# The skip term of a long convolution, moved from a matmul over channels to the diagonal of products that lie in SBUF

## What is computed

```python
kv = vr[:, :, :, None, :] * x2r[:, :, None, :, :]
y = irfft(rfft(kv, n=2*L) * rfft(k, n=2*L)[None, :, None, None, :], n=2*L)[..., :L]
skip = bias.reshape(H, num_heads)[None, :, :, None, None]
y = y + kv * skip
out = jnp.einsum('bhijl,bhil->bhjl', y, x1r)      # x1 = x2 = ctx
x = x + out.reshape(B, D, L)
```

## Time and profile before

| | |
|---|---|
| median of 3 runs | 1346.17 us |
| the profiled execution | 1338.81 us, of which its span 1337.0 us |
| mean granted TensorE clock | 0.946 of 2.4 GHz; 1.00 from 40 to 600 us |
| stage A | to about 620 us |
| busy over the span | TensorE 87%, VectorE 60%, GpSimd 51%, ScalarE 40% |

### The profile page before, as it was taken

The page is one execution under the profiler, slowest core; times in us unless marked ns, Lnnn a source line. Parts: engine busy times, 40 slices in busy tenths (PEclk is TensorE's granted clock), DMA queues, the critical chain, the costliest instruction groups (busy, mean ns, idle before and its releaser), DMA issues. The chain is left out here.

```text
span 1337.0 us, 18158 instructions
## 1 busy us (share of the span) xinstructions
PE 1165.7 (87%) x5305; PEld 881.9 (66%) x5305; DVE 799.4 (60%) x1240; ACT 533.2 (40%) x980; POOL 687.4 (51%) x388
## 2 busy tenths in 40 slices
PE   3999999999999999998689999998878787878770
PEld 2767777777777777766589899965545454545450
DVE  1687777877777877776579955535333343334340
ACT  5455555555555555543212122134323233323330
POOL 5987889888898888880000000022334443444432
PEclk9999999999999999999799999999888899889985
DMA  6222333233333223312483344459999999899973
GB/s 187 83 72 77 98 98 95 74 85 88 98 98 87 84 75 98 98 50 57 99 245 105 107 119 112 111 167 289 248 247 261 251 270 270 215 266 259 258 184 39
DMA packets 87546, 194.73 MB, mean 146 GB/s; under 512 B 17888, under 2 KB 22688, under 8 KB 87392
## 3 DMA queue, kind: packets, MB, share of 16 engines
q1 hardware_dynamic: 73184, 158.76, 39.9%
q0 software_dynamic: 14336, 35.66, 13.2%
HBM read 150.55 MB, written 43.79 MB: 145 GB/s over the span
## 5 line engine op out<-in xcount | busy, mean ns | idle before, releaser
L937 POOL TENSOR_TENSOR ring<-vT,cT 128x1024 f32<-128x1024 f32 x128 | 249.0, 1955 | 79.5 <-ACT vT L710 52.9
L390 PE MATMUL Y<-split,toep 128*128 128x512 f32 x576 | 250.4, 435 | 9.4 <-POOL split L945 9.4
L1056 DVE TENSOR_TENSOR z<-Y,cT 128x1024 f32<-128x1024 f32 x128 | 156.1, 1219 | 126.0 <-PE Y L394 90.3
L945 POOL TENSOR_TENSOR split<-ring,split 128x1024 fp32r<-128x1024 f32 x96 | 229.7, 2393 | 0.4 <-ACT split L720 0.4
L392 PE MATMUL Y<-split,toep 128*128 128x512 f32 x576 | 228.5, 397 | 0.0
L391 PE MATMUL Y<-split,toep 128*128 128x512 f32 x576 | 228.3, 396 | 0.0
L981 POOL DMA_INDIRECT stage<-xn_rows,idx_i x64 | 71.5, 1117 | 299.6 <-issue 282.4
L608 PE MATMUL Y<-ring,xT 128*128 128x384 f32 x512 | 209.8, 537 | 0.5 <-DMA ring<-in_L_ffn_down_proj_dram 0.5
L1061 DVE TENSOR_REDUCE o<-z 128x128 f32<-128x1024 f32 x128 | 154.4, 1206 | 1.1
L521 PE MATMUL Y<-split 128*128 128x384 f32 x768 | 152.2, 347 | 1.6 <-DVE split L1115 1.6
L390 PEld LDWEIGHTS Y<-split,toep 128*128 128x128 f32 x576 | 109.2, 190 | 39.5 <-issue 19.1
(11 more groups left out here) (135 smaller groups left out, 1736.4 us busy)
## 6 DMA issues: line engine op xcount, KB each, us to landing
ring<-_L_ffn_gate_up_proj_dram SPq DMA_DIRECT2D x64, 768.0 KB
ring<-in_L_ffn_down_proj_dram SPq DMA_DIRECT2D x64, 384.0 KB
gr<-filters SPq DMA_DIRECT2D x32, 512.0 KB, 3.7
stage<-in_x_dram SPq DMA_DIRECT2D x32, 256.0 KB, 3.5
stage<-in_ctx_dram SPq DMA_DIRECT2D x32, 256.0 KB, 3.7
x_rows<-stage SPq DMA_DIRECT2D x32, 256.0 KB, 2.9
xn_rows<-xn SPq DMA_DIRECT2D x32, 256.0 KB, 3.0
xn<-xn_rows SPq DMA_DIRECT2D x32, 256.0 KB, 3.7
```

The source lines that it names most:

```text
L390: pe.matmul(y, high, kv[:, s, 0, a, n], start=(a == 0), stop=False)
L937: pool.tensor_tensor(to.rearrange("p (b j i) -> p b j i", i=NH, j=NH), a, d, ALU.mult).then_inc(kvp_ready, 1)
L945: pool.tensor_tensor(kv[:, s, 1, c, :], kvp[c], kv[:, s, 0, c, :].bitcast(F32), ALU.subtract).then_inc(kv_ready, 1)
L1056: dve.tensor_tensor(zz[c % 2].rearrange("p (b j i) -> p b j i", j=NH, i=NH), YY[c % 2][:, :].rearrange("p (b j i) -> p b j i", j=NH, i=NH) ...
```

## The change

The skip sum is no longer made by TensorE. The products that GpSimd has already written to SBUF hold, at every ninth of 64 columns, the products with equal heads. VectorE multiplies these diagonals by the skip values, into `w` (`diagonals`, once for chunks 0 to 2 and once for chunk 3), sums each eight (`v_ctx`, now on VectorE), multiplies by `cT` (`skip_term`, now in SBUF) and adds the result to the whole of `o` before it is transposed (`add_skip`). GpSimd's `v_ctx`, ScalarE's `skip_block`, TensorE's skip matmul and VectorE's `residual` go. `xr` is loaded straight from `x` by a DMA (`load_residual`), together with the skip values, behind the two stores and so ahead of the next load of filters. `load_tile` waits for `cT_ps` in place of `xr_ready`. GpSimd's products wait for the diagonals of the tile before, since these read the buffers that it writes. The copy of `six_scores` becomes a multiplication by 1.0. The three product buffers are laid into one strided tensor.

```diff
+            def load_residual(h, s):
+                if not among(h, 0, 1):
+                    sp.wait_ge(x1_ready, h - 1)
+                load_skip(h, s)
+                sp.dma_start(xr[:, s, :], rows(x_f, h)).then_inc(xr_in[s], 16)
             def load_tile(h, s):
-                sp.wait_ge(xr_ready, h - 1)
+                sp.wait_ge(cT_ps, h - 1)
                 load_rows(h, s)
-                load_skip(h, s)
...                                                   (SyncE, iteration)
                     store(h - 1, 1 - s)
+                if not among(h, NT - 1):
+                    load_residual(h + 1, 1 - s)
...                                                   (TensorE, transposes, turn_o)
-                pe.wait_ge(w_ready, h + 1)
-                pe.wait_ge(skip_ready, h + 1)
-                pe.matmul(DX[:, :], skip_b[:, s, :], w[:, s, :], start=True, stop=True).then_inc(dx_ps, 1)
-                pe.wait_ge(o_done, h * NC + NC)
+                pe.wait_ge(o_whole, h + 1)
...                                                   (ScalarE)
-                act.activation(skip_b[:, s, :], same_b, ACT.Copy, scale=skip_c[:, s, :]).then_inc(skip_ready, 1)
...                                                   (GpSimd, product and v_ctx)
                     if not among(h, 0):
+                        pool.wait_ge(diag_ready, h * 2 - 1)
                         pool.wait_ge(kv_ready, (h - 1) * (NC - 1) + c + 1)
-                pool.tensor_tensor(w[:, s, :], v[:, s, :], ct[:, s, :], ALU.mult).then_inc(w_ready, 1)
...                                                   (VectorE)
+            def diagonals(h, s, last):
+                dve.wait_ge(kvp_ready, h * NC + (NC if last else NC - 1))
...
+                n, c = (1, NC - 1) if last else (NC - 1, 0)
+                products = kv3[s].unsqueeze(1) if last else kvp_all
+                products = products.rearrange("p c (b n) -> p c b n", b=B)[:, :, :, 0:NH * NH:NH + 1]
+                skips = skip_c[:, s, :].unsqueeze(1).unsqueeze(1).to_broadcast([P, n, B, NH])
+                dve.tensor_tensor(w[:, s, c * P:(c + n) * P].rearrange("p (c b i) -> p c b i", c=n, i=NH),
+                                  products, skips, ALU.mult).then_inc(diag_ready, 1)
+            def v_ctx(h, s):
+                dve.tensor_reduce(vct[:], w[:, s, :].rearrange("p (n i) -> p n i", i=NH), AX.X, ALU.add).then_inc(vct_ready, 1)
             def skip_term(h, s):
-                dve.tensor_tensor(DX[:, :], DX[:, :], ct[:, s, :], ALU.mult).then_inc(dc_ready, 1)
-            def residual(h, s):
-                dve.tensor_tensor(xr[:, s, :], DX[:, :], xt[:, s, :], ALU.add).then_inc(xr_ready, 1)
+                dve.tensor_tensor(w[:, s, :].rearrange("p (n i) -> p n i", i=NH),
+                                  cT[:, s, :, :].rearrange("p c (b i) -> p (c b) i", i=NH),
+                                  vct[:].unsqueeze(2).to_broadcast([P, NC * B, NH]), ALU.mult).then_inc(skip_ready, 1)
+            def add_skip(h, s):
+                dve.wait_ge(o_done, h * NC + NC)
+                dve.wait_ge(skip_ready, h + 1)
+                whole = o[:, s, :, :].rearrange("p c n -> p (c n)")
+                dve.tensor_tensor(whole, whole, w[:, s, :], ALU.add).then_inc(o_whole, 1)
...                                                   (VectorE, six_scores)
-                dve.tensor_copy(s6[:, 0:K], s8[:, 0:K]).then_inc(s6_ready, 1)
+                dve.tensor_scalar(s6[:, 0:K], s8[:, 0:K], 1.0, None, ALU.mult).then_inc(s6_ready, 1)
...                                                   (VectorE, iteration)
                     total(h - 1, 1 - s, 3)
+                    add_skip(h - 1, 1 - s)
                 times(h, s, 0)
                 if prev2:
                     best_scores(h - 2)
-                if nxt:
-                    skip_term(h + 1, 1 - s)
+                diagonals(h, s, False)
                 total(h, s, 0)
                 times(h, s, 1)
+                diagonals(h, s, True)
                 if prev2:
                     six_scores(h - 2)
                 if prev:
                     add_x1(h - 1, 1 - s)
-                if nxt:
-                    residual(h + 1, 1 - s)
...
+                v_ctx(h, s)
                 times(h, s, 2)
+                skip_term(h, s)
                 total(h, s, 2)
```

More of the change, by code:

```diff
@@ L95, in build @@
         kv = split[:].rearrange("p (s a c n) -> p s a c n", s=2, a=2, c=NC)
-        kvp = [ring[:, 3, 0:KVC], ring[:, 3, KVC:2 * KVC], ring[:, 0, SI * NC:]]
-        kv3 = [ring[:, 1, SI * NC:], ring[:, 2, SI * NC:]]
+        kvp_all = ring[:, 0:NC - 1, SI * NC:]
+        kvp = [kvp_all[:, n, :] for n in range(NC - 1)]
+        kv3 = [ring[:, 3, 0:KVC], ring[:, 3, KVC:2 * KVC]]
         z = sb("z", [P, 4, 512])
@@ L473, in iteration @@
                 if not among(h, 0):
-                    if not among(h, NT - 1):
-                        pe.wait_ge(xr_ready, h + 2)
-                    else:
+                    if not among(h, 1):
+                        pe.wait_ge(sc_ready, h - 1)
+                    if among(h, NT - 1):
                         pe.wait_ge(sh_lo, 2)
@@ L762, in iteration @@
                 if nxt:
-                    skip_block(h + 1, 1 - s)
                     filter_blocks(h + 1, 1 - s)
@@ L1061, in total @@
                 dve.tensor_reduce(o[:, s, c, :], zz[c % 2].rearrange("p (n i) -> p n i", i=NH), AX.X, ALU.add).then_inc(o_done, 1)
-            def skip_term(h, s):
-                dve.wait_ge(dx_ps, h + 1)
-                dve.tensor_tensor(DX[:, :], DX[:, :], ct[:, s, :], ALU.mult).then_inc(dc_ready, 1)
-            def residual(h, s):
-                dve.wait_ge(dc_ready, h + 1)
-                if not among(h, 0, 1):
-                    dve.wait_ge(x1_ready, h - 1)
-                dve.tensor_tensor(xr[:, s, :], DX[:, :], xt[:, s, :], ALU.add).then_inc(xr_ready, 1)
+            def diagonals(h, s, last):
+                dve.wait_ge(kvp_ready, h * NC + (NC if last else NC - 1))
+                if not last:
+                    dve.wait_ge(skip_in[s], landed(h, s, 16))
+                    if not among(h, 0, 1):
+                        dve.wait_ge(o_whole, h - 1)
+                n, c = (1, NC - 1) if last else (NC - 1, 0)
[4 more added lines that the diff above has]
+                                  products, skips, ALU.mult).then_inc(diag_ready, 1)
@@ new lines, in v_ctx @@
+            def v_ctx(h, s):
+                dve.wait_ge(diag_ready, h * 2 + 2)
+                if not among(h, 0):
+                    dve.wait_ge(skip_ready, h)
+                dve.tensor_reduce(vct[:], w[:, s, :].rearrange("p (n i) -> p n i", i=NH), AX.X, ALU.add).then_inc(vct_ready, 1)
+            def skip_term(h, s):
+                dve.wait_ge(vct_ready, h + 1)
+                dve.tensor_tensor(w[:, s, :].rearrange("p (n i) -> p n i", i=NH),
+                                  cT[:, s, :, :].rearrange("p c (b i) -> p (c b) i", i=NH),
+                                  vct[:].unsqueeze(2).to_broadcast([P, NC * B, NH]), ALU.mult).then_inc(skip_ready, 1)
@@ L1129, in iteration @@
                     best_scores(h - 2)
-                if nxt:
-                    skip_term(h + 1, 1 - s)
-                else:
+                diagonals(h, s, False)
+                if not nxt:
                     shared_low(0)
@@ L1168, in _ @@
                 shift1(h)
-                if h == 0:
-                    skip_term(0, 0)
-                    residual(0, 0)
             dve.wait_ge(small_in, 16)
@@ L1255, in _ @@
             total(NT - 1, 1, 3)
+            add_skip(NT - 1, 1)
             scores(NT - 2)
```

34 lines of the change are left out of this document (10 added, 24 removed).

## The result

| | us | to the kernel before |
|---|---|---|
| before | 1346.16 (median of 4) | |
| after | 1419.55 (median of 4, 1415.87 to 1421.73) | 1.0557 (1.0509 to 1.0605) |
| forecast | 1373 (1320 to 1398) | |

What follows compares the result with a forecast made beforehand. Stage A was taken as bounded by TensorE's list and VectorE's cycle with GpSimd port waits. 16.3 + 0.1 + 1.0 + 2.15 = 19.55, taken as 19.4 us against 18.5, +27 us over 30 tiles: 1373 us, range 1320 to 1398.

Steps and rivals of the forecast that it cites:

- the cycles: Stage A's two limits per tile: TensorE's list, 17.8 us falling to 16.95, and VectorE's, 19.48 falling to 16.3 without port waits.
- the port: VectorE instructions reading SBUF by two routes wait for GpSimd's running instruction to end; at most 2.4 us each.
- Rival 2: No lock for tensor_tensor: 16.95 to 17.7 us per tile, middle 1310 us; chance 0.17 together with late filters bounding stage A.
- rival 1: The lock holds but `six_scores` gets through: 18.1 to 18.8 us per tile, 1334 to 1356 us; chance 0.36.
- the price of the step: Extra VectorE time for diagonals reading one column in nine, bounded at 0 to 0.5 us per tile.
- `six_scores` in full: On VectorE, `six_scores` lets GpSimd go first and waits for a whole product or low part: 2.15 us.
- the wait of the second diagonals: VectorE's diagonals over 128 columns wait for GpSimd's first or second product: 1.0 us, between 0.2 and 1.9.
- the step of nine: VectorE's diagonals read one column in nine: 0.1 us per tile in the forecast, 0.5 kept for the range.
- the cycle as laid out: VectorE's cycle in stage A: 16.3 us without port waits, plus 0.1, 1.0 and 2.15, giving 19.55 us per tile.
- changing phases: Stage A's tile taken as 19.4 instead of 19.55 us, as phases would differ from tile to tile.
- a stall was priced at its length: TensorE idle ahead of L407 over 2 us per tile, with no added price for a slower clock.
- Filters: SyncE loads filters 1.3 us plus 0 to 1 us later, moving GpSimd's start to 5.4 to 6.4 us; no cost by itself.

Runs made afterwards that it cites:

- after_six_reduce: The changed kernel with `six_scores` made by a tensor_reduce over one element instead of the multiplication by 1.0: 1353.2 us, 1.006 to before.
- after_filled_stall: The changed kernel with twelve overwritten 512-column matmuls added ahead of `turn_xn`, where TensorE waits for `xn`: 1396.0 us, 1.035 to before.
- after_filters_first: The changed kernel with only SyncE's order changed, skip values and `xr` loaded behind the filters: 1409.7 us, 1.041 to before.

## Why the prediction was right and where it failed

**Right: the cycles.** The list of TensorE without the skip matmul, 16.95 us, was reached (16.9). That the copy of six columns holds the kernel before at 18.5 us was read from ends that coincide, and taking it out gave the 17.8 us of the undisturbed tile.

**Right: the port.** All of it was argued from one instruction of six columns. The experiments show it for tensor_tensor with two fp32 inputs in SBUF, by the operand (1777 to 393 ns) and by the moment (1616 to 389 ns), and show that the multiplication by 1.0 waits as the copy did. The rule of the Trainium skill that the prediction named ("SBUF — State Buffer", Who interferes with whom) agrees with the durations shown here, down to the blocked GpSimd instruction (2.85 us for 2.41). Rival 2, no lock, falls; rival 1, `six_scores` getting through, too. Its other half held once the instruction was mended: `after_six_reduce` had 18.8 us, rival 1 with the price of the step 18.7 to 18.8. That they meet so closely is in part luck: the 18.8 us contain the low clock of some tiles (granted clock 0.98 from 100 to 550 us), which rival 1 did not have either.

**Right: `six_scores` in full.** Forecast 2.15 us of wait, measured 2266 - 149 = 2.12 us.

**Mis-sized: the wait of the second diagonals.** Put at 1.0 us between bounds of 0.2 and 1.9; measured 1777 - 390 = 1.39 us. The middle of the bounds was no better than a guess, and hardly any tile had it: of the 24 tiles from 100 to 600 us, 19 took 1.94 to 2.06 us, one 1.46 and four 0.43 to 0.73. In the 19, GpSimd had started right behind the first diagonals and was at the start of its second product when VectorE asked (316.79 and 318.80 us in the timelines above); the list of waits has GpSimd held up by the diagonals 19 times.

**Mis-sized: the step of nine.** Put at 0.1 us, with 0.5 kept for the range; measured 0.35 + 0.12 = 0.47 us. The nearest row, ScalarE with a step of four, had said 1.0 ns for each column, and 0.9 ns it was. The row and the section that the prediction named ("Advanced Engine Details and Errata" of the Trainium skill, Memory Cachelines) both pointed to the upper end, and I took neither.

**The cycle redone.** With the measured means, 16.3 + 0.47 + 1.39 + 2.12 = 20.3 us. In the first tile of the view above (20.47 us) the two instructions took 2.04 and 2.35 us, so with its own waits the sum is 16.3 + 0.47 + 1.65 + 2.20 = 20.6 us. So the cycle as laid out holds to 0.2 us. The prediction further cut its 19.55 to 19.4 for changing phases; there was no row for that. Its upper bound of 20.3 us a tile was not the sum of its own upper prices either: 16.3 + 0.5 + 1.9 + 2.4 = 21.1 us, some 1424 us. A range up to there would have held the measured time, but by luck, with the term below still at nothing. The tiles of after at full clock took 20.0 us on average, so the terms above account for 0.6 us a tile, some 18 us of the 46 us by which the forecast was short.

**The step that failed: a stall was priced at its length.** The sum took a tile as the longer of two lists, and gave TensorE's standing still no price of its own. The profile before had stalls of up to 1.4 us, with a granted clock of 1.00 over two such tiles. The forecast itself made them over 2 us per tile, and at that point had left what the rows could vouch for. They became 3.4 us and more, and in 11 of 23 tiles the clock then stood at 1.2 GHz, for some 3.5 us in eight of them and 6.9 us in three. The tiles of 20.47 and 22.03 us, alike in the waits, differ by 1.56 us. In the 11, TensorE was busy 1.4 to 2.9 us longer than in the others, 20 us in sum or 0.9 us for each of the 23 tiles; and the mean of 21.1 us is 1.1 us over that of the 12 at full clock. So over 32 tiles the low clock comes to some 25 to 35 us (an estimate from these figures). `after_filled_stall` was 24 us faster, of which some 16 or more are left for the clock. Without the low clock after would have been at about 1385 to 1395 us, inside the range (the same estimate).

**Filters.** Forecast as 1.3 us later plus up to 1 us: ScalarE's wait grew by 1.8 us, and GpSimd started 5.8 us behind the `times` of chunk 3 (311.00 and 316.79 us), inside the 5.4 to 6.4 us of the forecast. That it cost nothing by itself in the changed kernel is shown by `after_filters_first` as far as the wait for `xn` goes (3.3 and 3.5 us a time).

**Still open.** Why the clock fell in some tiles and not in others. A tile of after that reached TensorE's stall at 285 us waited 3.38 us and ran on at full pace; the one at 324 us waited 3.40 us and did not. The first of them:

```profile
288.64 0.63 PE L410 MATMUL TA<-sq,xn 128*128 128x128 f32 x4 [3.38 <-ACT xn L724]
...
289.57 0.40 PE L395 MATMUL Y<-split,toep 128*128 128x512 f32 x1
289.81 0.39 PE L393 MATMUL Y<-split,toep 128*128 128x512 f32 x1
290.04 0.39 PE L394 MATMUL Y<-split,toep 128*128 128x512 f32 x1
```

In `after_filters_first` all stalls from 130 us on took 3.4 to 3.6 us, and the clock stayed at 1.00. A shorter stall can be enough, too: in `after_six_reduce` the 0.43 us pace followed five stalls of 2.36 to 2.48 us (134, 302, 377, 452 and 528 us) and did not follow three of 2.39 us (191, 228 and 265 us). The length of the single stall doesn't decide it.

## What to carry to other kernels

Before moving work to VectorE, list which of its instructions will have two inputs in SBUF, or copy from SBUF to SBUF, while GpSimd computes: each that asks during a GpSimd instruction waits for its end, and two of them in a row can cost a whole GpSimd instruction more. An operand in PSUM, a tensor_reduce in place of a small copy, or a place in GpSimd's gap takes the wait away. And when a forecast makes TensorE stand still for longer than any stall in the profile at hand, price the stall and the slower clock behind it.

## What the runs showed of the hardware that was not expected

- Work added in a stall made the kernel faster: 372 matmuls of 512 columns more, 24 us less, with the granted clock from 100 to 550 us at 1.00 instead of 0.95.
- A stall of 3.40 us was followed by the low clock, one of 3.38 us, 39 us earlier, was not; in another kernel five stalls of 2.36 to 2.48 us were.
- A copy of six columns cost 1.9% of the kernel before: 24 us by 32 instructions. In after, a multiplication of six columns in its place cost 66 us.
- Reading every ninth fp32 column on VectorE costs 0.9 ns per column more, 883 against 535 ns for 384 columns.
- GpSimd waits in its turn: its low part took 2.85 instead of 2.41 us when it started beside a VectorE product of 512 columns.
